# A Flamingo-style attention and mixture-of-experts kernel: TensorE's filler transpositions between the last router product and the first gate product are left out

## What is computed

```
x = x + tanh(g_xattn[0]) * L0_xattn(layernorm(x), ctx)     # 16 heads of 16, layernorm of q and k
x = x + tanh(g_ffn[0])   * tanh(layernorm(x) @ W0 @ W1 @ W2 + bias)
x = x + tanh(g_xattn[1]) * L1_xattn(layernorm(x), ctx)     # 8 heads of 64, keys from x and ctx
x = x + tanh(g_ffn[1])   * L1_ffn(layernorm(x))
```

```
probs = softmax(x @ gate_w.T); w, idx = top_k(probs, 2); w = w / sum(w)
for each of 8 experts:
    g, u = split(x @ gup.T, 2)               # gup: 2048 x 256
    acc += combine[:, e] * (silu(g) * u @ dn.T)   # dn: 256 x 1024
```

## Time and profile before

| | us |
|---|---|
| three timed runs | 587.49, 587.41, 585.88 (median 587.41) |
| the profiled execution, its own time | 586.68 |
| span of the profiled execution | 584.8 |
| TensorE busy (share of the span) | 560.3 (96%) |
| VectorE busy | 405.9 (69%) |
| ScalarE busy | 311.8 (53%) |
| GpSimd busy | 274.9 (47%) |
| mean granted clock of TensorE | 0.996 of full |

### The profile page before, as it was taken

How to read it: one execution, slowest core, us unless ns; L and a number is a source line. 1 busy time by engine, 2 the same in 40 slices (tenths; PEclk the granted TensorE clock), 3 DMA queues, 4 the chain that set the end, 5 groups by cost and what they waited for, 6 DMA issues and landing times.

```text
span 584.8 us, 13702 instructions
## 1 busy us (share of the span) xinstructions
PE 560.3 (96%) x5606; PEld 484.8 (83%) x5606; DVE 405.9 (69%) x817; ACT 311.8 (53%) x602; POOL 274.9 (47%) x237
## 2 busy tenths in 40 slices
PE   8999999999979999999999999998899999999994
PEld 8777677777657788989888888977899999979994
DVE  7877658678667666877767767677677677746652
ACT  3545554554645456555555556553565656636631
POOL 3736647757740164666655466631202334421424
PEclk9999999999999999999999999999999999999998
DMA  7910840000000000000000000008573567726112
GB/s 255 359 43 2 328 181 3 1 3 2 2 2 1 2 1 2 9 17 9 18 8 19 9 26 13 13 16 346 164 251 127 180 222 252 242 47 235 26 22 25
DMA packets 24091, 50.93 MB, mean 87 GB/s; under 512 B 7072, under 2 KB 17104, under 8 KB 20688
## 3 DMA queue, kind: packets, MB, share of 16 engines
q1 hardware_dynamic: 18560, 45.20, 21.5%
q0 software_dynamic: 4224, 3.70, 3.6%
q10 hardware_dynamic: 1232, 1.01, 0.6%
HBM read 37.89 MB, written 13.31 MB: 88 GB/s over the span
## 4 chain that ended last, share of the span: by engine, by line
PE 86%; DVE 5%; POOL 3%; issue 2%; ACT 1%; DMA 1%; POOLq 0%; DVEq 0%; ACTq 0%
PE ps L59 15%; PE ps L60 14%; PE ps L61 14%; PE ps L740 5%; PE ps L758 5%; PE ps L728 4%; PE ps L595 4%; PE ps L613 4%; DVE KN L1127 3%; PE ps L629 3%; PE ps L685 2%; PE ps L675 2%; POOL sr L1829 2%; PE ps L503 2%; PE ps L806 2%
## 5 line engine op out<-in xcount | busy, mean ns | idle before, releaser
L1886 POOL TENSOR_SCALAR P<-P,rinv 112x487 f32<-112x487 f32 x56 | 84.8, 1525 | 46.9 <-DVE rinv L1160 46.8
L1127 DVE TENSOR_REDUCE KN<-ps 112x4 f32<-112x1500 f32 x32 | 55.0, 1720 | 31.1 <-PE ps L595 30.8
L61 PE MATMUL ps<-XGf,WL 128*128 128x256 f32 x252 | 71.3, 283 | 0.0
L60 PE MATMUL ps<-XGf,WH 128*128 128x256 f32 x252 | 71.3, 283 | 0.0
L59 PE MATMUL ps<-XGf,WH 128*128 128x256 f32 x252 | 71.3, 283 | 0.0
L1829 POOL TENSOR_TENSOR sr<-sv,mhalf 125x32 f32<-125x32 f32 x13 | 70.7, 5441 | 1.1
L412 POOL DMA_INDIRECT out<-WS,rows_i x16 | 28.4, 1776 | 89.0 <-ACT WS L1732 85.7
L1485 DVE TENSOR_TENSOR WL<-WR,WH 128x1024 fp32r<-128x1024 f32 x48 | 57.1, 1220 | 13.9 <-ACT WH L1786 10.3
L1648 ACT ACTIVATE P<-ps,nm 112x487 f32<-112x487 f32 x64 | 41.9, 665 | 34.9 <-DVE nm L1152 33.8
L1599 ACT ACTIVATE P<-ps 125x1344 f32<-125x1344 f32 x32 | 41.4, 1292 | 35.0 <-PE ps L613 34.6
L1786 ACT ACTIVATE WH<-WR 128x1024 fp32r<-128x1024 f32 x48 | 48.7, 1049 | 0.0
(11 more groups left out here) (271 smaller groups left out, 1516.8 us busy)
## 6 DMA issues: line engine op xcount, KB each, us to landing
WR<-in_gupT SPq DMA_DIRECT2D x16, 1024.0 KB, 7.1
WR<-in_dwnT SPq DMA_DIRECT2D x8, 1024.0 KB, 10.4
xs<-ZT SPq DMA_DIRECT2D x14, 516.0 KB, 6.0
CT<-in_ctxT SPq DMA_DIRECT2D x1, 2250.0 KB, 11.7
P<-xs SPq DMA_DIRECT2D x7, 256.0 KB, 10.6
P<-xs SPq DMA_DIRECT2D x9, 128.0 KB, 2.4
Wk<-in_L_xattn_Wk SPq DMA_DIRECT2D x2, 512.0 KB, 11.2
Wv<-in_L_xattn_Wv SPq DMA_DIRECT2D x2, 512.0 KB, 11.1
```

Of the source, the lines that this page charges most:

```text
L60: e.matmul(out, ah, bl, start=False, stop=False)
L61: return e.matmul(out, al, bh, start=False, stop=stop)
L1127: e.tensor_reduce(heads(KN[b % 2][0:NQ, 3, :])[:, 4 * k:4 * k + 4, 16], ps[0:NQ, 0:4, 0:NC], AX.X, ALU.max, negate=True).then_inc(s("smax" ...
L1886: e.tensor_scalar(P[:, k, 0:487], P[:, k, 0:487], rinv[:, k:k + 1], None, ALU.mult).then_inc(s("psc"), 1)
```

## The change

Two entries of the table of fillers are taken out, with the bank that one of them wrote. The other four stay.

```
-WARM = {("kp", 0, 1, 0): 36, ("spk", 0, 2): 24, ("xt", NB - 1, 3): 18, ("rt4", NB - 1): 26, ("xin", 0): 62,
-        ("up", 0, 0): 10}
-
-WARM_BANK = {("up", 0, 0): 5}
+WARM = {("kp", 0, 1, 0): 36, ("spk", 0, 2): 24, ("xt", NB - 1, 3): 18, ("rt4", NB - 1): 26}
+
+WARM_BANK = {}
```

## The result

The changed kernel takes 589.47 us (median of 20 runs, 588.68 to 592.44) against 587.52 us for the kernel before on the same chips (20 runs, 585.88 to 588.86). The medians lie 1.95 us apart, where 2.0 us was forecast. The ratio, which is not formed from these two medians, is 1.0038 with a 95% interval of 1.0028 to 1.0048, that is 2.2 us (1.6 to 2.8). The profiled execution of the changed kernel has a span of 588.2 us and took 590.03 us, and is thus one of the slower of the 20.

What follows compares the result with a forecast made beforehand. The prediction took TensorE to bound the kernel. From a start of 587.0 us it added 1.7 us for slow products and 0.3 us for a later first gate product, 2.0 us in all, giving 589.0 us, range 586.9 to 590.8.

Steps and rivals of the forecast that it cites:

- What bounds: Whole kernel, mainly behind 423.3 us: TensorE bounds it, so any delay there moves the end by as much.
- (1): Before the turns: removing the 62 fillers brings the gather no sooner, gain 0; TensorE is left idle for 8.1 us.
- (2): Idle wait before the turns: the clock falls to half by 421.83 us, as it fell 3.3 us after the program's end.
- (3): Products at half clock: 0.21 to 0.23 us each instead of 0.120, losing 0.45 of each slow microsecond.
- (4): Behind the first gate product: the slow stretch lasts 3.7 us, a loss of 1.7 us.
- (5): From the turns to the first gate product: slow turns, with the ten fillers' gain included, make it 0.3 us later.
- A: Behind the first gate product: full clock returns within 3 us, loss below 1.7 us, 587.5 to 588.7 us; chance 0.31.
- B: At the turns: the clock is still full, so the kernel is not slower, 585.9 to 587.0 us; chance 0.07.
- C: Behind the first gate product: products stay slow for long, ten slow microseconds in all giving 591.8 us; chance 0.05.
- D: In the experts: a DMA or another engine bounds, TensorE's slack absorbs the loss, 0 to 0.3 us, 587.0 us; chance 0.05.

Runs made afterwards that it cites:

- ten_doubled: Kernel before with 20 instead of ten fillers between the turns and the first gate product; 587.91 us, ratio 1.0019.
- early40: Kernel before with 40 of the 62 fillers kept, right behind the last router product, and the ten out; 589.22 us, ratio 1.0030.
- early22: Kernel before with 22 of the 62 fillers kept, right behind the last router product, and the ten out; 589.04 us, ratio 1.0031.
- none_late: Kernel before with all four late filler groups (18, 26, 62 and ten) out; 589.46 us, ratio 1.0041.
- after_again: The changed kernel run once more, without the 62 and the ten fillers, against the kernel before; 588.91 us, ratio 1.0032.
- only62: Kernel before with the 62 fillers ahead of the turns kept and the ten behind them out; 587.16 us, ratio 1.0006.

## Why the prediction was right, point by point

- **What bounds.** Right. No wait of TensorE behind 430 us came or went, and ten_doubled prices a delay at 423 us with all of its 1.1 us.
- **(1), the 62 at gain 0.** Nearly right. The scatter takes 2.58 us instead of 2.60, and the gather 2.54 instead of 2.42 us, within 0.01 us of the longest with all 62 fillers (2.53). But the first turn begins 0.14 us behind the gather instead of 0.04 in every profile without fillers ahead of it. So 0.10 us was put at nothing: either the bank waits or the long wait itself costs it.
- **(2), the fall of the clock.** Right in all four profiles without fillers ahead of the turns. The 3.3 us from the last work to the fall, taken from the program's end, was one sample: in the seven profiles with an idle time of 3.2 us or more late in the program it is 2.2 to 5.1 us. The 8.1 us left room for that. In early40, with 3.0 us of idle time, the fall came 4.0 us after the last filler, behind the turns. The Trainium skill's example of a wait of 8 us that leaves TensorE cold (TensorE: Matmul & The Clock Gate, "Loop structure matters more than you think") holds here with 8.49 us and 0.50.
- **(3), the price.** The slow product takes 0.213 us, at the lower end of the 0.21 to 0.23 taken, and the same as the estimate from the Trainium skill (the same page, "Wait — 56ns, not 53.3ns?"). The loss for each slow microsecond was 2.07 / 5.0 = 0.41, 1.24 / 3.0 = 0.41, and 0.43 in early22 (2.63 / 6.2), against the 0.45 taken.
- **(4), the length.** This is the least certain term. I took 3.7 us; the profiles show 5.0, 3.0, 6.2 (early22) and 4.6 us (none_late, 423.59 to 428.2), 4.7 on the mean, and the two of the changed kernel itself 4.0. Only one of the four is under the 3.7. The choice was made from a single start of the program. The statement of the Trainium skill (TensorE: Matmul & The Clock Gate, "What's actually happening") that the count of cold matmuls differs from run to run is borne out here behind a wait: the same kernel had 5.0 and 3.0 us.
- **(5), turns and ten.** 0.27 us, where 0.3 was taken. VectorE's part of the tokens was not waited for, as forecast. The ten's gain of 0.15 us, seen with the 62 in place, is real only up to the next wait, which I had not priced.
- **Sum.** From the changed kernel's two profiles 0.27 + 4.0 x 0.41 + 0.10 = 2.0 us, from all four 0.27 + 4.7 x 0.42 + 0.10 = 2.3 us; forecast 2.0, measured 1.95 by the medians and 2.2 by the ratio. With slow stretches of 3.0 to 6.2 us in single executions, an agreement to 0.05 us is partly luck. The time itself was forecast as 589.0 us and is 589.47: the start of 587.0 us, taken from four executions, was 0.5 us under the median of 587.52.
- **Rivals.** A is one end of the same thing (after_again, 1.5 us). B, C and D did not occur in any profile: the clock never held through the 8 us, never stayed low for over 7 us behind the gate product, and ten_doubled leaves no slack for D. One of the 20 runs took 592.44 us, more than C's 591.8, and has no profile.

## What to carry to other kernels

A bound TensorE that waits for a DMA pays twice: the wait, and then half clock on the work behind it. Fillers in the wait cost nothing as long as they run at full clock and end before the data arrives. Covering the whole wait saved the loss; a part of it did so less surely, whether early (22 saved nothing, and with 40 the clock fell behind the wait) or late (ten saved most of the loss on the median and failed in five of twelve runs). Price the fillers at half clock as well, since a group that just fits at full clock delays the data's user when the clock has fallen (26 took 4.70 us instead of 3.04).

## What the runs showed that I had not expected

- The clock can fall after the wait is over: in early40 it was full through 3.0 us of idle time and the four turns, and fell at 424.9 us, in the 0.69 us of pause ahead of the products. In only62 it fell at 411.0 us, under fillers that had run for 1.0 us. A gap is not safe because the work right behind it runs at full clock.
- By its mean clocks the kernel before has such a fall in about a quarter of its runs (23 of 86), with 1.3 us between the medians; only62 and early40 show it in a profile among the router products. The one profile that was shown ahead of the prediction had none.
- Half clock in a stretch of waits is nearly free: 10 us more of it in none_late added nothing that can be measured. With fillers in that stretch it is not: the 26 then took 1.66 us more and held up the last router product.
